# A mixing product ahead of the gate turn in each first-stage step, and the upper parts first in the first expert slot

## The reference

```python
att = softmax(gelu(gelu(cond @ W0 + b0) @ W1 + b1) @ W2 + b2)            # 32 samples x 8 kernels
agg_w = einsum('bk,koi->boi', att, weight)                               # a 64x64 matrix per sample
c0 = einsum('boi,bih->boh', agg_w, x) + (att @ bias_k)[:, :, None]       # the mixing
logits = einsum('bsh,he->bse', c0, gate_w)                               # gate, 8 experts
topv, topi = top_k(logits, 2);  w = softmax(topv)
x = x + sum over the two experts e in topi of w_e * (c0 @ expert_w[e])
```

## Time and profile before

| | us |
|---|---|
| median of 3 runs | 807.54 (807.08 to 810.27) |
| the profiled execution | 806.61 |
| its span, first to last instruction | 804.9 |
| TensorE busy in the span | 780.9 (97%) |
| VectorE busy in the span | 393.6 (49%) |
| one step of the first stage, 44.49 to 51.91 | 7.42 |

### The profile page before, as it was taken

One profiled execution on the slowest core, in us unless ns is written; L12 is line 12 of the kernel. 1 busy time (PEld: TensorE's weight loads), 2 busy tenths in 40 slices (PEclk: granted clock), 3 DMA queues, 4 the chain that ended last, 5 costly groups with the idle time before them and its releaser, 6 DMA issues.

```text
span 804.9 us, 13018 instructions
## 1 busy us (share of the span) xinstructions
PE 780.9 (97%) x4426; PEld 635.9 (79%) x4426; DVE 393.6 (49%) x920; ACT 206.3 (26%) x324; POOL 84.7 (11%) x127
## 2 busy tenths in 40 slices
PE   6999899899999999999999999999999999999997
PEld 4555587678787787877878888878988889889886
DVE  2688642330422413214133153475777667778883
ACT  3444152341523314224133251300000010001200
POOL 1000202001110110001011112211111111200000
PEclk9999999999999999999999999999999999999999
DMA  9997397376482765726455355774445654442066
GB/s 349 388 372 264 126 375 259 113 252 244 177 308 95 243 268 196 277 97 224 148 174 199 104 196 175 240 190 115 104 108 143 144 126 104 113 98 52 1 221 197
DMA packets 62880, 152.51 MB, mean 189 GB/s; under 512 B 7148, under 2 KB 24700, under 8 KB 61948
## 3 DMA queue, kind: packets, MB, share of 16 engines
q1 hardware_dynamic: 43152, 99.84, 38.0%
q0 software_dynamic: 9504, 34.48, 14.0%
q10 hardware_dynamic: 10188, 17.71, 5.9%
HBM read 99.04 MB, written 44.57 MB: 178 GB/s over the span
## 4 chain that ended last, share of the span: by engine, by line
PE 90%; DMA 5%; issue 2%; ACT 1%; DVE 1%; SPq 1%; POOLq 0%; POOL 0%; ACTq 0%; DVEq 0%
PE bank L1498 61%; PE bank L1586 6%; PE bank L1595 4%; PE bank L1393 3%; PE bank L1489 3%; PE bank L1541 3%; PE bank L1602 3%; DMA work<-c_scratch,idx 3%; PE bank L1370 1%; PE bank L1417 1%; PE bank L1552 1%; DMA work<-y_scratch,pos_c 1%; DMA x1p<-res 1%; PE bank L1356 1%; PE bank L1382 1%
## 5 line engine op out<-in xcount | busy, mean ns | idle before, releaser
L1498 PE MATMUL bank<-weights,l_hi 128*128 128x512 f32 x1536 | 473.5, 389 | 0.0
L1498 PEld LDWEIGHTS bank<-weights,l_hi 128*128 128x128 f32 x1536 | 288.4, 188 | 58.3
L1498 PE MATMUL bank<-weights,l_lo 128*128 128x512 f32 x768 | 304.7, 397 | 1.1 <-DVE l_lo L1086 1.1
L1498 PEld LDWEIGHTS bank<-weights,l_lo 128*128 128x128 f32 x768 | 144.2, 188 | 34.0 <-issue 6.2
L1086 DVE TENSOR_TENSOR l_lo<-bank,l_hi 128x512 fp32r<-128x512 f32 x32 | 22.2, 693 | 174.7 <-ACT l_hi L797 174.7
L1118 DVE TENSOR_TENSOR weights<-work,weights 128x1024 fp32r<-128x1024 f32 x48 | 55.9, 1221 | 33.9 <-ACT weights L809 33.9
L1586 PE MATMUL bank<-conv_sb,x1p 128*128 128x128 f32 x512 | 59.8, 275 | 2.7 <-DMA x1p<-res 1.6
L1586 PEld LDWEIGHTS bank<-conv_sb,x1p 128*128 128x128 f32 x512 | 58.7, 192 | 3.2 <-DMA x1p<-res 1.8
L1240 DVE TENSOR_TENSOR res<-bank,res 128x512 f32 (+1 forms) x30 | 31.9, 1064 | 54.8 <-PE bank L1498 43.8
L648 POOL DMA_INDIRECT work<-c_scratch,idx x32 | 33.4, 1045 | 227.1 <-PE bank L1489 138.8
L888 ACT ACTIVATE l_hi<-work 128x512 fp32r<-128x512 f32 x32 | 18.4, 623 | 135.4 <-PE bank L1498 129.2
(11 more groups left out here) (204 smaller groups left out, 603.6 us busy)
## 6 DMA issues: line engine op xcount, KB each, us to landing
work<-in_expert_w SPq DMA_DIRECT2D x52, 512.0 KB, 5.4
y_scratch<-work ACTq DMA_DIRECT2D x64, 256.0 KB, 3.4
x1p<-in_expert_w SPq DMA_DIRECT2D x20, 512.0 KB, 8.3
y_scratch<-ca SPq DMA_DIRECT2D x19, 512.0 KB, 10.1
res<-in_x SPq DMA_DIRECT2D x16, 512.0 KB, 11.2
c_scratch<-work SPq DMA_DIRECT2D x16, 512.0 KB, 5.0
res<-in_x_ph SPq DMA_DIRECT2D x14, 512.0 KB, 5.8
x1p<-res SPq DMA_DIRECT2D x112, 64.0 KB, 4.7
```

Of the source, the lines that this page charges most:

```text
L1498: mm = pe.matmul(to[:, :], a[:, k, :], b[:, k, cols * HALF:(cols + 1) * HALF], start=(k == 0 and n == 0), stop=(k == HC - 1 and n == 2 and ...
```

## The change

Two edits, both in TensorE's stream. In steps 1 to 6, `mix(it, 0, 0)` is issued before `turn_gate(it)` and not after it. In the first slot of expert 0, the left half is done by `first_left_half()`: the products of `l_hi` first, those of `l_lo` after them, by groups of four blocks, each behind its own semaphore. The number of products is the same, as are the transfers and the other engines' streams.

```diff
-                turn_gate(it)
+                if it == 0 or last:
+                    turn_gate(it)
                 mix(it, 0, 0)
+                if 0 < it and not last:
+                    turn_gate(it)
...
+            def first_left_half():
+
+                for blocks, upper, lower in ((range(0, 4), s_ha, s_la), (range(4, HC), s_hb, s_lb)):
+                    pe.wait_ge(upper, 1)
+                    for k in blocks:
+                        for n, part in enumerate((w_hi[0], w_lo[0])):
+                            pe.matmul(bank[0][:, :], l_hi[:, k, :], part[:, k, 0:HALF], start=(k == 0 and n == 0), stop=False)
+                    pe.wait_ge(lower, 1)
+                    for k in blocks:
+                        mm = pe.matmul(bank[0][:, :], l_lo[:, k, :], w_hi[0][:, k, 0:HALF], start=False, stop=(k == HC - 1))
+                return mm
...
+                mm = first_left_half() if first and isinstance(e, int) and e == 0 else left_half(g, odd)
```

More of the change, by code:

```diff
@@ L1500, in product, with left_half @@
                 return mm
[L1502 to L1506, removed]
+            def left_half(g, odd):
                 pe.wait_ge(s_la, g + 1)
@@ L1511, in slot @@
                     mm = product(k, bank[0], w_hi[odd], w_lo[odd], 0)
+                return mm
[8 more added lines that the diff above has]
+                        mm = pe.matmul(bank[0][:, :], l_lo[:, k, :], w_hi[0][:, k, 0:HALF], start=False, stop=(k == HC - 1))
+                return mm
+            def slot(g, e, odd, first):
+                if first:
+                    pe.wait_ge(s_lo, (e + 1) * HC)
+                pe.wait_ge(s_e0, g + CREDIT)
+                mm = first_left_half() if first and isinstance(e, int) and e == 0 else left_half(g, odd)
                 mm.then_inc(s_h0, 1)
```

## The result

| | before | after |
|---|---|---|
| median of 10 runs, us | 809.64 (806.39 to 810.65) | 804.2 (801.72 to 807.6) |
| the profiled execution | 806.61 | 804.94 |
| its span | 804.9 | 803.2 |

The ratio after to before is 0.9942, with a 95% interval of 0.9924 to 0.9961. Two more sets of runs of the same changed kernel, against runs of the kernel before on the same chip, gave 0.9974 (0.9955 to 0.9993) and 0.9963 (0.9936 to 0.9989). The mean of the three ratios is 0.996, 3.3 us: faster, by a little less than the first set says. The record shows the runs of the kernel before that stood beside the later sets: 35 with a median of 809.20 beside r1 to r4, and 19 with 808.39 beside r9 to r12. The ratios are the record's; those of the bare medians differ from them by up to 0.16% (r10 has 0.9966, and 804.32 to 808.39 is 0.995).

What follows compares the result with a forecast made beforehand. The prediction took the loop of TensorE and VectorE, 7.42 us a step, as the first stage's bound, and TensorE's pace elsewhere. Savings of 2.4 + 0.6 = 3.0 us from 807.54 gave 804.5 us, range 803.3 to 806.6.

Steps and rivals of the forecast that it cites:

- the sum: Whole kernel: 2.4 us from the first stage's steps and 0.6 from the first expert slot, 3.0 us in all.
- The signs: Trace readings named beforehand: steps of 6.95 to 7.05 us, first product 0.7 to 0.8 after ScalarE's upper part starts.
- The places: TensorE's waits for VectorE: once per first-stage step, in a loop of 7.42 us, and once at the first expert slot.
- Edit 1, TensorE's side: First-stage steps: the moved mixing product fills a 0.59 us hole; TensorE's step falls by 0.51 us to 6.91.
- Edit 1, VectorE's side: First-stage steps: VectorE's idle 0.38 us before line 961 goes; its step becomes 6.97 to 7.04 us, saving 2.4 in all.
- Rival (a): First-stage steps give the whole hole, 3.1 us, and the slot 0.7: 3.8 us, total 803.7; chance 0.15.
- Which engine is the bound: First-stage steps after the change: VectorE bounds, and about 0.1 us of TensorE's gain is left as a wait.
- The cover of the gate turn: First-stage steps: the turn is delayed 0.35 us, yet its result comes 0.04 us before VectorE needs it.
- rival (c): First-stage steps: transfers at 362 GB/s are the floor, 1.1 us from steps and 0.6 from the slot, 805.8; chance 0.04.
- Rival (d): First-stage steps: the moved mixing product waits for its bank, despite 1.7 us of slack; slower, 812 us; chance 0.05.
- Edit 2: First expert slot: products start behind ScalarE's upper part with 0.14 us of issue; gain 0.6 us, bounds 0 and 0.7.
- rival (b): Register loads or the gather hold TensorE at the first slot, gain 0; late gate turn leaves steps 2.0, 805.5; chance 0.14.

Runs made afterwards that it cites:

- r1: Kernel before with only the mixing product moved ahead of the gate turn in steps 1 to 6, first slot as before: 806.95 us, ratio 0.9967.
- r4: Kernel before, unchanged, run again for a second profile and more times: 808.51 us, ratio 0.9996.
- r9: Changed kernel with both mixing products of tile 0, not one, ahead of the gate turn in steps 1 to 6: 808.28 us, one execution; regular steps 7.33 to 7.35.
- r12: Changed kernel, unchanged, run a third time: 805.46 us, ratio 0.9963.
- r10: Changed kernel with one TensorE register load ahead of the first transposes, in place of two loads: 804.32 us, ratio 0.9966.
- r2: Kernel before with only the first slot's left half reordered, upper parts first, steps as before: 808.29 us, ratio 1.0001.
- r5: Kernel before with an unused reduction over 256 columns added on VectorE in steps 1 to 6: steps 7.42 us, unchanged; 806.66 us, one execution.
- r7: Kernel before with an unused 128x128 product on TensorE ahead of the gate turn in steps 1 to 6: steps 7.42 us, unchanged; 809.37 us, one execution.
- r6: Changed kernel with an unused reduction over 256 columns added on VectorE in steps 1 to 6: steps 7.16 us against 6.84; 805.67 us, one execution.
- r8: Changed kernel with an unused 128x128 product behind the third mixing product of steps 1 to 6: steps 7.06 to 7.07 us; 804.63 us, one execution.
- r3: Changed kernel, unchanged, run again for a second profile and more times: 807.03 us, ratio 0.9974.
- r11: As r10, with the mixing product ahead of the gate turn in the last step too: 803.64 us, ratio 0.9947.

## Why the prediction was right

Forecast 804.5 us, 3.0 less than the 807.54 of before; measured 804.2 in the first set, and 3.3 us less in the mean over three sets. The two places give 3.2 + 0.34 = 3.5 us in the profiles, for the 2.4 + 0.6 of the sum: one term was too small, one too large, and the errors cancel in part. That the 804.2 lies so near the 804.5 is luck. In that set the kernel before had 809.64 us and not 807.54, and the saving was 4.7 us by the ratio.

**The signs.** Two of the numbers that were to show it right were not met. The steps are 6.84 us and not 6.95 to 7.05, and the first product of the first slot starts 1.12 us after ScalarE's upper part does (88.31 to 89.43), not 0.7 to 0.8. The idle times before lines 961 and 1382 are gone, as it said, and there is none before line 966.

**The places.** Right. r1 and r2 put the gain into the steps, and r5 and r7 show that before the change both engines had room in a step, as the loop through both requires.

**Edit 1, TensorE's side.** The hole of 0.59 us was filled as said, and the product costs 0.94 us where it stands. The term that was too large is the gate turn: 0.44 us was its spacing behind a wait; behind a running product it is 0.36. So TensorE's step is 6.91 - 0.08 = 6.83 us, measured 6.84.

**Edit 1, VectorE's side.** The mechanism was right and the size too small. The idle 0.38 us went, and the 0.08 of overlap before line 961 came on top, which the 2.4 counted in part. What I didn't see is a third saving: the rank products start 0.34 us after line 961 and not 0.44. Before, line 1409 started 0.03 us behind line 961, and the rank products wait for its result: they start 0.41 us after it. Now line 1409 starts 0.08 us ahead of line 961, with the same 0.42 to the rank products. In r6 it starts 0.7 us ahead, and the spacing of VectorE's two lines is still 0.33, so that is VectorE's own. 7.42 - 0.38 - 0.08 - 0.10 = 6.86, measured 6.84. Rival (a), the whole hole, is thus what happened in the steps: 44.46 - 41.25 = 3.2 us between line 961 of step 1 and of step 7, where the forecast had 2.4 and the rival 3.1. Its objection, that VectorE's instructions don't shrink, was true and not enough, for their starts moved together.

**Which engine is the bound.** Half wrong. I said VectorE, with a tenth left for TensorE; r8 shows that TensorE has nothing left, r6 that VectorE hasn't either.

**The cover of the gate turn.** Right, and tighter than is comfortable: the turn at 44.83 in step 3 of the changed profile, 1.09 us after line 961, and VectorE takes its result at 45.44 without idle time, 0.61 us after the turn started. It is 0.61 to 0.62 in r9 too, where VectorE waits for it, so the result comes just as it is wanted. r9 shows what is behind the edge.

**Transfers, rival (c).** Wrong as a bound in the regular steps. The rows after have 372 GB/s over 30 us, above the 362 of the rows before. The Trainium skill's "DMA: Bandwidth & Descriptors", section "Where 436 GB/s comes from", has 358 for a core; the trace disagrees, with the 372. The steps ask for more still, and what let them run is the slack of the loads, as the prediction had it. The rival had a point at a place that I had costed at nothing, the start. I had worked out the slack of the last load only, 13.6 us; in r3 the load of step 2 was issued at 18.46 and its gate products waited for it until 34.49. That cost 1.45 us there, and 0.32 in r10.

**Rival (d), the bank.** It did not happen in the steps of the first profile, though ScalarE's waits for the stores rose from 3.3 us in one case to 13.7 in four; the slack of 1.7 us covered them. It happened once in each of the four profiles of the new order that start step 1 by 27.4 us (r3, r6, r9 and r10), with 0.35 to 0.45 us, and not in r4, which starts as early in the old order. The sum for the slack took the hole of 0.6 us off twice, since 51.3 is the product's start without the hole already (51.10 and 0.22). In the changed profile the eviction starts at 48.21 and the product that needs its first half at 50.73.

**Edit 2.** The step that failed is the 0.14 us of issue, behind which rival (b) had put the register loads. I took it from before the change, where VectorE's part came later than the register loads, and read it as a sign that the loads were long done. They were not: they ended some 0.4 us after ScalarE's part (0.52 - 0.14), as r10 shows by moving one ahead and leaving the other out. The gain was 0.34 of the forecast 0.6. The picture in the Trainium skill's "Perfetto Trace Analysis", section "Tensor Engine Instruction (MATMUL, LD_WEIGHTS)", by which a matmul waits in a queue while the sequencer decodes on, gave 0.68. The trace disagrees with what I made of it: there are 0.52 us of issue with the loads behind the transposes, which wait for the gather, and 0.14 with the load ahead of them. Whether the loads began only when the transposes had started, or began earlier and took that long, no run tells.

**The chances.** Within 0.5% had 0.86, and faster by more than that 0.09. The first set came out at 0.58%, with an interval from 0.39 to 0.76, on the side of the 0.09; the other two sets have 0.26 and 0.37.

**Carried to the end.** From line 961 of step 1 to the second slot's transposes it is 94.98 - 30.01 = 64.97 us, and 97.53 - 28.87 = 68.66 before: 3.7 us less. From the same line to the end of the span it is 2.8 us less (773.19 against 776.03). The wait near 133, 2.20 us against 0.97, took more than the difference, and that wait differs as much between profiles of one kernel.

## What to carry to other kernels

Where two engines wait for each other once in every step, neither is the bound, and work that is independent of the exchange should stand in the wait: first measure the hole from start to start, then check how far the delayed hand-over may slip before the other engine notices. The gain is what the engine with less room has left, and small overlaps at semaphores that are no longer waited for come on top. A wait whose length fits the semaphore says nothing of what would come next if it went: look at every instruction between the wait and the one before it, register loads too.

## What the runs showed of the hardware

**The granted clock falls in some executions only.** In r1, r9 and r12, all with the new order of the steps, it was 0.83 from 88 to 98 us, behind TensorE's wait for the first gather; the five profiles with the old order have 1.00 there. Elsewhere it fell in r3 (0.57 from 36 to 44), in r6 (0.61 from 72 to 76, behind 1.03 us without work) and, with the old order, in r4 (0.83 from 26 to 36). The window of r12:

```profile
88.00:98.00 10.00, 8.93 (x39) 7.29 (x40) 4.89 (x18) 1.78 (x4) 1.33 (x3) 0.83 0.34 114
```

and the products in it, on TensorE's timeline:

```profile
90.13 3.25 PE L1520 MATMUL bank<-weights,l_hi 128*128 128x512 f32 x8 [0.72 <-ACT l_hi L797]
```

Eight products take 3.25 us and not 2.08, at 1.2 GHz in part; the slot is 1.6 us longer (8.92 against 7.34). The length of the wait ahead doesn't decide it: it was 1.18 to 1.28 us in the three with the fall, and 1.42 in the first profile of the changed kernel and 1.44 in that of before, without it.

**The new order doesn't lower the clock more often.** The record has the mean granted clock of each execution. It is 0.999 or 1.000 in 16 of 34 executions of the changed kernel and in 28 of 66 of the kernel before (those beside the later sets, and r4's). Their medians are 804.10 and 808.21 us, 4.1 apart; the others' are 807.12 and 809.84, 2.7 apart. So the sets scatter with the clock, and the gain is clearest where it is full. In r10 and r11 it is full in 13 of 14 executions, which may be chance; whether the shorter wait in the first slot does it (0.34 us against 0.72), no run tried.

**Transfers beside each other.** The wait for the fifth slot's gather, near 133 us, was 0.7 to 3.1 us over these profiles, with no relation to the edits.
